# Another order of work inside the groups of an attention loop: heads' low halves first, quotients, residual, layer norm and router steps in portions behind

## What is computed

```python
ln = layernorm(layernorm(x)); xn = layernorm(ctx)      # ctx: 64 rows of 192 per sequence
q = ln @ Wq.T
kv = concat([xn @ Wkv.T, ln @ Wlkv.T])                 # 64 + 1024 keys
qn, kn = rmsnorm(q) * SCALE, rmsnorm(k)                # per head of 64
attn = softmax(where(mask, qn @ kn.T, -big))
x = x + tanh(g_xattn) * ((attn @ v) @ Wo.T + bo)
y = layernorm(x)
probs = softmax(y @ w_router); topk_w, topk_idx = top_k(probs, 2)
h = gelu(einsum('te,ieh->tih', y, w1) + b1)
x = x + tanh(g_ffn) * sum_over_top2((h @ w2 + b2) * weights)
```

## Time and profile before

| | |
|---|---|
| timed runs | 1117.05, 1120.57, 1120.69 us (median 1120.57) |
| the profiled execution | 1114.85 us, span 1113.0 us, mean granted clock 0.932 |
| attention loop in it | 62.12 to 606.91 us of the span |
| tail | 606.91 to 678.00 us |
| experts | 678.00 to 1113.0 us |
| busy share of the span | PE 88%, DVE 52%, ACT 43%, POOL 29% |

### The profile page before, as it was taken

The page is one execution under the profiler, slowest core; times in us unless marked ns, Lnnn a source line. Parts: engine busy times, 40 slices in busy tenths (PEclk is TensorE's granted clock), DMA queues, the critical chain, the costliest instruction groups (busy, mean ns, idle before and its releaser), DMA issues. The chain is left out here.

```text
span 1113.0 us, 19158 instructions
## 1 busy us (share of the span) xinstructions
PE 980.0 (88%) x5932; PEld 756.2 (68%) x5932; DVE 575.2 (52%) x1562; ACT 475.3 (43%) x909; POOL 319.1 (29%) x279
## 2 busy tenths in 40 slices
PE   3689899898998998989999506999999999999991
PEld 3555455564555554555644406999999999999991
DVE  5315435456444554544443452676675757666651
ACT  4244464344543454533442113446454545454440
POOL 3232121112161212442105061233333333342231
PEclk8579999999999998999999657999999999999996
DMA  4010010100110100211002153352534243552225
GB/s 113 1 40 1 0 41 0 39 1 1 40 62 16 38 1 14 98 42 39 1 1 77 38 148 114 47 128 41 124 74 100 40 127 47 128 123 43 47 35 163
DMA packets 44984, 62.06 MB, mean 56 GB/s; under 512 B 7280, under 2 KB 38768, under 8 KB 44880
## 3 DMA queue, kind: packets, MB, share of 16 engines
q0 software_dynamic: 17520, 33.27, 13.8%
q1 hardware_dynamic: 27376, 26.20, 8.3%
q10 hardware_dynamic: 48, 2.10, 0.6%
HBM read 37.34 MB, written 28.39 MB: 59 GB/s over the span
## 5 line engine op out<-in xcount | busy, mean ns | idle before, releaser
L1173 PE MATMUL psO<-p_ring,V 128*128 128x512 f32 x576 | 273.1, 606 | 0.8 <-ACT o_sb L606 0.8
L617 ACT ACTIVATE p_ring<-psS,shift 128x1024 f32<-128x1024 f32 x128 | 136.7, 1112 | 183.4 <-PE psS L1160 183.4
L1482 PE MATMUL psH<-xT_hi,Q 128*128 128x256 f32 x1120 | 203.4, 281 | 1.6 <-DVE xT_lo L1399 1.6
L1495 PE MATMUL psY<-K,g_hi 128*128 128x256 f32 x1120 | 203.4, 284 | 0.0
L1335 POOL DMA_INDIRECT total<-y_out,token_i x70 | 116.3, 1662 | 253.4 <-DVE y_out L1420 241.5
L481 POOL TENSOR_TENSOR rr<-ssm,minus_half 128x4 f32<-128x4 f32 (+1 forms) x72 | 70.4, 977 | 395.6 <-DVE ssm L715 395.6
L1482 PEld LDWEIGHTS psH<-xT_hi,Q 128*128 128x128 f32 x1120 | 174.2, 189 | 2.0 <-issue 2.0
L1495 PEld LDWEIGHTS psY<-K,g_hi 128*128 128x128 f32 x1120 | 171.7, 188 | 0.0
L1173 PEld LDWEIGHTS psO<-p_ring,V 128*128 128x128 f32 x576 | 103.7, 194 | 94.5 <-issue 92.8
L1495 PE MATMUL psY<-K,g_lo 128*128 128x256 f32 x560 | 157.3, 281 | 0.0
L1482 PE MATMUL psH<-xT_lo,Q 128*128 128x256 f32 x560 | 157.0, 280 | 0.0
(11 more groups left out here) (188 smaller groups left out, 1154.6 us busy)
## 6 DMA issues: line engine op xcount, KB each, us to landing
lnf<-routed SPq DMA_DIRECT2D x35, 258.0 KB, 2.8
xr<-in_L_ffn_w POOLq DMA_DIRECT2D x7, 1024.0 KB, 6.1
xn<-in_L_ffn_w POOLq DMA_DIRECT2D x7, 1024.0 KB, 8.7
xr<-in_x SPq DMA_DIRECT2D x4, 1024.0 KB, 5.1
total<-xb SPq DMA_DIRECT2D x4, 1024.0 KB, 4.4
routed<-pad_rows SPq DMA_DIRECT2D x8, 258.0 KB, 4.9
total<-y_out,token_i POOLq DMA_INDIRECT x70, 3.9
routed<-big,slot_i POOLq DMA_INDIRECT x64, 2.7
```

The source lines that it names most:

```text
L617: act.activation(p_ring[0:p, u % RING, :], psS[u % 2][0:p].rearrange("p a n -> p (a n)"), ACT.Exp, bias=bias).then_inc(exp_done, 1)
L1173: ins = pe.matmul(psO[odd][:], V[:, (w % 2) * KT + kt, odd * DH:odd * DH + P], p_ring[:, u % RING, odd * HALF:(odd + 1) * HALF], start=(kt ...
L1482: ins = pe.matmul(o, l, r, start=(n == 0), stop=(n == len(parts) - 1))
L1495: ins = pe.matmul(psY[m][:, 0:D], l[:, c, cols], r[:, c, :], start=(c == 0 and n == 0), stop=(c == HC - 1 and n == 2))
```

## The change

Nothing that is computed changes; instructions are put in another order on four engines. On DVE, `heads_lo` comes first in each group, then `mean_squares` and `scale_heads`, and the rest stands behind them: `quotients` of the window before are spread over `i = 0` and `i = 1` and those of the window itself move from `i = 6, 7` to `i = 5, 6`; `second_stats` go to `i = 2, 3`, `normed_rows` to the end of `i = 4`; the next sequence's `norm_stats` and `norm_variance` move a window ahead (odd windows, `i = 7, 8`); `norm_rows` to `i = 7, 8`; the router's steps one to two groups later. On ACT, `heads_hi` goes ahead of `read_projection`, `norm_hi` ahead of `take_even`. On PE, `turn_heads` goes ahead of `project`; the `turn` uses are gathered in `i = 6, 7` and `logits` goes to `i = 8`. On POOL, `norm_root` moves to `i = 0`, `second_root` and `second_rows` one group later. Cut to its core:

```diff
@@ mid_uses
-                    if i in (4, 6):
-                        return [("turn", b - 1, 0 if i == 4 else 3)]
+                    if i in (6, 7):
+                        return [("turn", b - 1, 2 * (i - 6))]
@@ late_uses
-                    if i in (4, 5):
-                        return [("turn", b - 1, i - 3)]
-                    if i == 6:
+                    if i in (6, 7):
+                        return [("turn", b - 1, 2 * (i - 6) + 1)]
+                    if i == 8:
                         return [("logits", b - 1)]
@@ POOL
-                        if b >= 1 and i == 3:
+                        if b + 1 < B and i == (4 if b == 0 else 0):
+                            norm_root(b + 1)
+                        if b >= 1 and i == 4:
                             second_root(b - 1)
-                        if b >= 1 and i == 4:
+                        if b >= 1 and i == 5:
                             second_rows(b - 1)
-                        if b + 1 < B and i == 7:
-                            norm_root(b + 1)
@@ ACT
+                    if w % 2 == 1 and b >= 1 and i == 0:
+                        router_exp(b - 1)
                     if i == 5:
                         take_even(2 * w)
+                    if turned_at(g) is not None:
+                        heads_hi(turned_at(g))
                     if tile_at(g) is not None:
                         read_projection(tile_at(g))
-                    if turned_at(g) is not None:
-                        heads_hi(turned_at(g))
+                    if w % 2 == 1 and b + 1 < B and i < 5:
+                        norm_hi(b + 1, i)
                     if i == 0 and w >= 1:
                         take_even(2 * w - 1)
-                    if w % 2 == 1 and b + 1 < B and i < 5:
-                        norm_hi(b + 1, i)
@@ DVE, ahead of the tile's steps
-                    if i == 1 and w >= 1:
-                        for odd in range(2):
-                            quotients(2 * w - 1, odd)
-                    if even and past and i == 4:
-                        for part in range(2):
-                            normed_rows(b - 1, part)
-                    if even and more and i in (5, 6):
-                        norm_stats(b + 1, i - 5)
+                    if not even and past and i == 0:
                         router_logits(b - 1)
+                    if not even and past and i == 1:
+                        router_softmax(b - 1)
+                    if not even and past and i == 5:
+                        router_slots(b - 1)
@@ DVE, the tile's steps and behind them
-                    if tile_at(g) is not None:
-                        mean_squares(tile_at(g))
                     if turned_at(g) is not None:
                         heads_lo(turned_at(g))
                     if tile_at(g) is not None:
+                        mean_squares(tile_at(g))
                         scale_heads(tile_at(g))
                     if even and past and i < 4:
                         residual(b - 1, i)
                     if i == 0 and w >= 1:
                         take_odd(2 * w - 1)
                     if not even and more and i < 5:
                         norm_lo(b + 1, i)
+                    if i < 2 and w >= 1:
+                        quotients(2 * w - 1, i)
+                    if i in (5, 6):
+                        quotients(2 * w, i - 5)
+                        if i in (2, 3):
+                            for q in range(2 * i - 4, 2 * i - 2):
+                                second_stats(b - 1, q)
+                        if i == 4:
+                            for part in range(2):
+                                normed_rows(b - 1, part)
+                        if i in (2, 3):
+                            router_largest(b - 1, i - 2)
+                        if i == 3:
+                            router_rows(b - 1)
@@ PE, tile_steps
+                    if turned_at(g) is not None:
+                        turn_heads(turned_at(g))
                     if tile_at(g) is not None:
                         project(tile_at(g))
-                    if turned_at(g) is not None:
-                        turn_heads(turned_at(g))
```

More of the change, by code:

```diff
@@ L630, in _ @@
                     b = w // 2
[L631 to L634, removed]
+                    if w % 2 == 0 and b >= 1 and i in (7, 8):
+                        turned_rows(b - 1, 2 * (i - 7) + 1)
                     for u in (2 * g, 2 * g + 1):
                         probabilities(u)
+                    if w % 2 == 1 and b >= 1 and i == 0:
+                        router_exp(b - 1)
                     if i == 5:
                         take_even(2 * w)
+                    if turned_at(g) is not None:
+                        heads_hi(turned_at(g))
                     if tile_at(g) is not None:
                         read_projection(tile_at(g))
-                    if turned_at(g) is not None:
-                        heads_hi(turned_at(g))
+                    if w % 2 == 1 and b + 1 < B and i < 5:
+                        norm_hi(b + 1, i)
                     if i == 0 and w >= 1:
                         take_even(2 * w - 1)
-                    if w % 2 == 1 and b + 1 < B and i < 5:
-                        norm_hi(b + 1, i)
[L647 to L650, removed]
+                    if w % 2 == 0 and b >= 1 and i in (6, 7):
+                        turned_rows(b - 1, 2 * (i - 6))
                 take_even(2 * WINDOWS - 1)
@@ L923, in _ @@
                     even, past, more = w % 2 == 0, b >= 1, b + 1 < B
-                    if i == 1 and w >= 1:
-                        for odd in range(2):
-                            quotients(2 * w - 1, odd)
-                    if even and past and i == 4:
-                        for part in range(2):
-                            normed_rows(b - 1, part)
-                    if even and more and i in (5, 6):
-                        norm_stats(b + 1, i - 5)
-                    if even and past and i == 7:
-                        router_logits(b - 1)
[L935 to L948, removed]
+                    if not even and past and i == 0:
+                        router_logits(b - 1)
+                    if not even and past and i == 1:
+                        router_softmax(b - 1)
+                    if not even and past and i == 5:
+                        router_slots(b - 1)
                     if i == 5:
                         take_odd(2 * w)
-                    if tile_at(g) is not None:
-                        mean_squares(tile_at(g))
                     if turned_at(g) is not None:
@@ L963, in _ @@
                         take_odd(2 * w - 1)
[L964 to L973, removed]
                     if not even and more and i < 5:
                         norm_lo(b + 1, i)
-                    if not even and past and i == 0:
-                        router_largest(b - 1, 0)
+                    if i < 2 and w >= 1:
+                        quotients(2 * w - 1, i)
+                    if i in (5, 6):
+                        quotients(2 * w, i - 5)
+                    if even and past:
+                        if i in (2, 3):
+                            for q in range(2 * i - 4, 2 * i - 2):
+                                second_stats(b - 1, q)
+                        if i == 3:
+                            second_variance(b - 1)
+                        if i == 4:
+                            for part in range(2):
+                                normed_rows(b - 1, part)
+                    if even and more:
+                        if i == 7:
+                            mask_to_bias(b + 1)
+                        if i in (7, 8):
+                            norm_rows(b + 1, i - 7)
+                    if w == 0 and i in (1, 2):
+                        norm_stats(1, i - 1)
+                    if w == 0 and i == 3:
+                        norm_variance(1)
+                    if not even and past:
+                        if i in (2, 3):
+                            router_largest(b - 1, i - 2)
+                        if i == 3:
+                            router_rows(b - 1)
+                    if not even and b + 2 < B:
+                        if i == 7:
+                            for part in range(2):
+                                norm_stats(b + 2, part)
+                        if i == 8:
+                            norm_variance(b + 2)
                 take_odd(2 * WINDOWS - 1)
```

## The result

The changed kernel takes 1071.4 us (median; 1070.99 to 1071.87), the kernel before in the same job 1118.8 (1116.8 to 1120.7). The ratio is 0.9577, with a 95% interval of 0.9554 to 0.9600. The profiled execution took 1070.99 us, with a span of 1069.1.

What follows compares the result with a forecast made beforehand. PE was taken to bound the attention loop, stalled by DVE's order. Stalls of 39.7 us less a new 1.2 us gave 38.5 us off 1114.85, 1076.4; with 4.0 us carried over, 1080.4 us, range 1073 to 1097.

Steps and rivals of the forecast that it cites:

- What bounds the loop, and that the stalls at `i = 1` and `i = 4` go: Attention loop: PE bounds it; DVE's order causes stalls, 32.5 us at `i = 1` and 5.5 us at `i = 4`, that go.
- The new wait behind the router step: `i = 1` of windows 3 and 5: `router_softmax` ahead of the tile makes PE wait 0.62 us, about 1.2 us in all.
- The add on POOL beside `norm_lo`: Windows 3 and 5: POOL's add holds `norm_lo` until 9.2 us, yet the next low halves precede the mid use by 0.3 us.
- a sign of being wrong: Waits of PE for `qkd` or for the bank at `project` would show the forecast wrong; no size given.
- They agree to 0.02 us where nothing is idle: Loop groups issuing the same work take equal time without idle: 6.48 us plain, 7.04 with `norm`, 8.37 with `out`.
- I take 0: PE's gap at the first 128-row matmul behind 64-row scores moves to the transposes: 0 us, bounds -2 and +6.
- The 4.0 us carried from the profiled execution to the median: Timed runs before lay 2.2 (lowest) and 5.7 us (median) above the profiled execution; the mean, 4.0, was added to 1076.4.
- The clock behind the logits: Group behind `logits`, now at `i = 8`: 1.5 us lost to lower clock is kept, bounds 0 and 4.6 us.
- more than forecast: Rival: no new stall, no clock lost after `logits`, none of the 4.0 us carried: 1073.7 us; chance 0.10 for below 1075.
- The idle time didn't move: Rival: idle time goes from DVE's queue to another resource of the same groups, time stays near 1118 us; chance 0.04.
- `turn_heads` ahead of `project` never waited: Slower rival: PE needs the scaled tile 1.15 us earlier and stands in each of 62 groups, up to 1130 us; chance 0.03.
- the partial return of the stalls: Rival: tight DVE sums in odd windows fail, half of the 32.5 us at `i = 1` stays, 1097 us; chance 0.15.

## Why the prediction was right and wrong

- *What bounds the loop, and that the stalls at `i = 1` and `i = 4` go.* Right. The six `i = 1` groups took 76.67 us before and take 45.07 now; the three at `i = 4` take 6.44 each, their `turn` blocks having moved. The waits at `i = 1` were an order on DVE; the runs with the quotients alone and without them show it from both sides. At `i = 4` the stalls are gone, but which of two moves did it isn't shown.
- *The new wait behind the router step.* Right in place, cause and size: 0.62 forecast, 0.68 measured, gone when the step was moved away.
- *The add on POOL beside `norm_lo`.* Right. The changed kernel has a sharper case of it: an instruction of 0.69 us took 1.81 and ended 0.55 us behind the add. The rule of the Trainium skill, page "SBUF — State Buffer", section "Who interferes with whom", that the one that comes second waits for the other's end, is borne out by this row. For the low halves of the next group the margin held. But the late `norm_lo` held `project` at `i = 2`, a wait that the prediction had named as a sign of being wrong: those groups take 6.91 us, and 6.74 where `norm_lo` ends earlier (low halves late again), 0.5 us in the three windows. That `quotients` could be held too wasn't seen.
- *The step that failed: "They agree to 0.02 us where nothing is idle", taken for "nothing is lost".* The groups without idle time went into the sum at their length of before, and the runs show two things in that length that the change takes away: waits for the low halves that are drawn as busy, and a price of PE's order, put at 0. Nor do the groups agree to 0.02 us: `norm` groups without idle time took 7.04 to 7.12 us, `out` groups 8.37 to 8.40.
- *The waits drawn as busy.* The two kinds of the earlier trace rows with a mid use, 7.04 and 8.37, were themselves held up. In the earlier trace rows, L736 ends at 409.94 + 0.28 = 410.22, and the mid use starts at 410.28; the same 0.06 us lie between the two at every open stall. So PE waited there, with no idle time shown, and so in all `norm` and `out` groups at `i = 0` and `3`; only at `i = 2` low halves ended some 0.5 us ahead of the mid use. In the changed kernel low halves end earlier, and the weight load can start ahead of the transposes:

```profile
250.65 0.59 PEld L1070 LDWEIGHTS psF<-ident,xn 128*128 128x128 f32 x4 [0.43 <-DVE K L734]
...
250.88 0.60 PE L1070 MATMUL psF<-ident,xn 128*128 128x128 f32 x4
```

  Before, both started at 410.28. From the first `values` to the mid use it is now 1.71 us for 1.83, and through the transposes 0.44 for 0.49.
- *"I take 0" for PE's order, bounds -2 and +6.* The run with this order undone puts it at about 4.4 us: 0.04 to 0.05 us in most of the 62 groups with tile steps, and 0.3 to 0.4 in the six at `i = 2`. It lies well outside the bound of -2, and I had put more room on the other side.
- *The terms.* Against the kinds used in the forecast (and what it kept for the router step and the clock), eight `norm` groups gained 1.4 us, twelve `out` groups 2.9, the nine with `turn` or `logits` 1.0, the 25 plain ones 0.9, window 7 0.3: 6.5 in all, which is the loop's 6.7 us to 0.2. With 4.4 us for PE's order, about 2 are left for the waits drawn as busy. Tail, experts and the loop's start were 1.3 us slower. So the profiled execution came out 5.4 us below the 1076.4 of the sum.
- *The 4.0 us carried from the profiled execution to the median.* Before, the median lies 4.0 us above it, now 0.4. That made 3.6 of the 9.0 us between 1080.4 and 1071.4. That executions of before differ by clock lost behind the stalls is argued from their profiles, not shown for the timed ones.
- *The clock behind the logits.* Kept at 1.5 us, which is what the profiled execution had; the bounds 0 to 4.6 were needed, for it had 0, 1, 2 or 3 such groups in different executions.
- *The rivals.* The time fell where "more than forecast" has it, below 1075 (chance 0.10), but not by its conditions: the new stall and the clock behind the logits stayed, only most of the 4.0 us carried fell away, and the 6.5 us of shorter groups aren't in it. So no rival of the prediction names what happened. The idle time didn't move, `turn_heads` ahead of `project` never waited, and the partial return of the stalls, with 0.15, drew the range to the wrong side: its upper part was unused while the low end was short by 1.6 us.

## What to carry to other kernels

When an engine that isn't the bound serves several streams, put first what the bound engine waits for in the same round, and spread long optional blocks behind it. Then follow every reader of a bank, not only the longest chain: here the low halves were in time and `norm_lo` wasn't. Before taking a group "without idle time" as the floor, compare the end of what it depends on with its start, and look whether the weight load starts ahead of the matmul or with it: a wait of 0.1 to 0.3 us can stand in every round and be drawn as busy. And leave room below the forecast when a change brings every dependency forward.

## What the runs showed of the hardware

- The clock fell behind a stretch of small matmuls, without any idle time. 32 matmuls of 8 columns in one piece of about 3.5 us were followed by a slow group (0.68 to 0.80 in the rows above) in nine of ten profiled executions; in two pieces of 1.8 us with 1.8 us of wide matmuls between, in none of the three places of one profiled execution.
- A matmul that waits for a semaphore held its weight load back too. In `out` groups of the kernel before, the low halves ended 1.70 to 1.73 us behind the start of the first `values`, just when the mid use can start at the earliest (1.71 in the changed kernel). The mid use started 0.06 us later, its load with it, and it took 1.83 us to the next `values`; with the load issued 0.43 us ahead it took 1.73. With the low halves at 1.85 the whole came to 0.31 us (8.47 for 8.16).
- Behind the scores, which use 64 rows, `project` ahead of the transposes cost 0.05 us more than behind them (6.48 for 6.44); behind `values`, which use 128, the order made no difference (6.49 and 6.49). Why it cost 0.3 us and more at `i = 2` stays open.
- In all four kernels run in one job, PE stood for 2.8 to 3.5 us at the end of the loop, with ACT's last exponentials 5.0 to 5.7 us apart. ACT's timeline of the one with the router step at `i = 0`, and of the changed kernel:

```profile
555.65 1.11 ACT L617 ACTIVATE p_ring<-psS,shift 128x1024 f32<-128x1024 f32 x1 [6.46 <-remote]
560.66 1.11 ACT L617 ACTIVATE p_ring<-psS,mask_bias 64x1024 f32<-64x1024 f32 x1 [3.89 <-remote]
```

The changed kernel:

```profile
554.82 1.11 ACT L617 ACTIVATE p_ring<-psS,shift 128x1024 f32<-128x1024 f32 x1 [3.09 <-PE psS L1159]
555.83 1.10 ACT L617 ACTIVATE p_ring<-psS,mask_bias 64x1024 f32<-64x1024 f32 x1
```

  In the first the scores of the group began at 551.28 and its two exponentials are 5.0 us apart; in the second they began at 553.82, and the two follow each other. The same program had none of it in its repeat in another job, so it isn't the change. Its cause stays open.
